# A decoder layer on one core: in the last group of the first attention, the bias, value and class products take earlier places in a hand-written order, and batch 1's middle stage moves up by 3.5 steps

## The reference, cut to what matters

```python
# first attention: classes of distance, 129 of them
dist = jnp.clip(idx[None, :] - idx[:, None], -R, R) + R        # R = 64
score = einsum('bhqd,bhkd->bhqk', q, k) + einsum('bhqd,qkd->bhqk', q, rel_emb_k[dist])
attn = softmax(score)
ctx = einsum('bhqk,bhkd->bhqd', attn, v) + einsum('bhqk,qkd->bhqd', attn, rel_emb_v[dist])
x = x + ctx @ W_out + b_out
x = x + memory_step(ctx_1024, layernorm(x))      # shifts, a convolution over 32 rows
# second attention and experts, on layernorm(x)
attn = softmax(rope(q) @ rope(k).T / sqrt(8));  x = rmsnorm(src + (attn @ v) @ Wo)
out = rmsnorm(x + shared + routed)
```

## Time and profile before

| | |
|---|---|
| time, median of 3 runs | 416.89 us (415.85 to 416.91) |
| the profiled execution: its time | 416.28 us |
| its span, first to last instruction | 414.5 us |
| mean granted TensorE clock | 0.916 |
| PE / DVE / ACT / POOL busy | 358.4 / 297.3 / 232.7 / 162.2 us |

### The profile page before, as it was taken

The page is one execution under the profiler, slowest core; times in us unless marked ns, Lnnn a source line. Parts: engine busy times, 40 slices in busy tenths (PEclk is TensorE's granted clock), DMA queues, the critical chain, the costliest instruction groups (busy, mean ns, idle before and its releaser), DMA issues.

```text
span 414.5 us, 12788 instructions
## 1 busy us (share of the span) xinstructions
PE 358.4 (86%) x5267; PEld 189.2 (46%) x5267; DVE 297.3 (72%) x538; ACT 232.7 (56%) x489; POOL 162.2 (39%) x342
## 2 busy tenths in 40 slices
PE   7776889898999999897889898768989898899993
PEld 4243456665676667664555332311233333453441
DVE  5996956777778788788799789566787661436465
ACT  2724665777676666665744567455767695422200
POOL 7263655465477576554470111200001161143423
PEclk9885558999999999999999699965999899999999
DMA  7400000000000001000000000500000000000000
GB/s 227 140 22 5 4 4 4 6 4 7 21 9 3 8 6 27 6 6 2 3 5 2 4 24 2 156 10 1 2 2 1 2 3 2 0 1 2 0 26 25
DMA packets 11991, 8.08 MB, mean 19 GB/s; under 512 B 4446, under 2 KB 11022, under 8 KB 11806
## 3 DMA queue, kind: packets, MB, share of 16 engines
q1 hardware_dynamic: 11934, 7.27, 6.1%
HBM read 5.94 MB, written 0.52 MB: 16 GB/s over the span
## 4 chain that ended last, share of the span: by engine, by line
PE 58%; DVE 21%; issue 7%; ACT 5%; SPq 3%; POOL 3%; DMA 2%; ACTq 0%; POOLq 0%; DVEq 0%
PE ps L1214 8%; PE ps L1309 7%; PE ps L1128 6%; PE ps L1159 5%; PE ps L1177 5%; PE ps L1186 4%; DVE m_qk L851 4%; PE ps L1201 4%; PE ps L1140 3%; PE ps L1004 3%; PE ps L1098 3%; DVE m_qk L848 2%; ACT arena L684 2%; PE ps L1295 2%; SPq L384 2%
## 5 line engine op out<-in xcount | busy, mean ns | idle before, releaser
L848 DVE TENSOR_REDUCE m_qk<-ps 128x2 f32<-128x1024 f32 x64 | 76.5, 1219 | 18.7 <-PE ps L1098 18.5
L851 DVE TENSOR_REDUCE m_qk<-ps 128x2 f32<-128x1024 f32 x64 | 76.9, 1219 | 16.1 <-PE ps L1186 15.7
L684 ACT ACTIVATE arena<-ps 128x512 f32<-128x512 f32 x128 | 69.4, 595 | 26.9 <-PE ps L1140 26.2
L699 ACT ACTIVATE arena<-ps 128x512 f32<-128x512 f32 x128 | 67.2, 591 | 21.3 <-PE ps L1201 21.0
L599 POOL TENSOR_TENSOR arena<-arena,eb 128x256 f32<-128x256 f32 x64 | 46.9, 733 | 60.6 <-ACT arena L684 31.5
L672 ACT ACTIVATE eb<-ps 128x512 f32<-128x512 f32 (+1 forms) x64 | 31.3, 542 | 28.0 <-PE ps L1128 28.0
L442 POOL TENSOR_SCALAR var<-mv 128x1 f32<-128x1 f32 (+1 forms) x14 | 2.7, 191 | 106.5 <-ACT eb L741 70.0
L1214 PE MATMUL ps<-arena,v_sb 128*20 128x256 f32 x512 | 41.2, 414 | 2.5 <-DVE arena L856 2.4
L1159 PE MATMUL ps<-arena,v_sb 128*20 128x128 f32 x1024 | 40.3, 284 | 0.0
L600 POOL TENSOR_TENSOR arena<-arena,eb 128x192 f32<-128x192 f32 x64 | 38.5, 602 | 0.0
L1201 PE MATMUL ps<-q_op,k_op 50*128 50x512 bf16 x128 | 31.9, 414 | 4.7 <-ACT arena L699 4.0
(11 more groups left out here) (217 smaller groups left out, 539.7 us busy)
## 6 DMA issues: line engine op xcount, KB each, us to landing
rel_v<-in_relv_ext SPq DMA_DIRECT2D x1, 1024.0 KB, 8.8
eb<-in_w SPq DMA_DIRECT2D x2, 512.0 KB, 5.6
x_sb<-in_x SPq DMA_DIRECT2D x2, 256.0 KB, 3.2
q_op<-farT SPq DMA_DIRECT2D x32, 3.0 KB
q_op<-farT SPq DMA_DIRECT2D x32, 1.5 KB
out<-x_sb SPq DMA_DIRECT2D x8, 64.0 KB, 1.5
rows<-in_rows SPq DMA_DIRECT2D x1, 448.0 KB, 6.6
sel<-in_sel SPq DMA_DIRECT2D x1, 384.0 KB, 4.2
```

What stands on the lines that cost most here:

```text
L684: act.activation(p_ring[:, k % SLOTS_P, e, :], ps[:, bank, :], ACT.Exp).then_inc(sm["bank_free"], 1)
L699: act.activation(p_ring[:, v % RING, e, :], ps[:, bank, :], ACT.Exp).then_inc(sm["bank_free"], 1)
L848: dve.tensor_reduce(m_qk[:, u, n:H:PAIRS], ps[:, banks, :], AX_X, ALU.max).then_inc(sm["pair_free"], 1)
L851: dve.tensor_reduce(m_qk[:, IT * b + n, 2 * p:2 * p + 2], ps[:, banks, :], AX_X, ALU.max).then_inc(sm["pair_free"], 1)
```

## The change

Only due times change; no instruction is added or removed, and the work of each item is as it was. For the last group (u = 7, start at step 84), `bias` items 1 to 3 come at 93.5, 95 and 96.5 in place of 95, 98 and 101; its eight `pv` at 106.5 to 110 in place of 108 to 112; its `crel` at 110.6 to 113 in place of 113 to 116; `ctx`, `turn`, `fin`, `norm`, `back` at 113.6, 114.2, 114.8, 116, 117.5 in place of 117, 117.6, 118.2, 119.5, 121. For the group before it (u = 6), `crel` comes at 102.3, 103, 103.7, 104.4 in place of 103 to 106, and `ctx` at 105.4 in place of 107. Batch 1's middle stage begins at 118.5 in place of 122, and its `max2` at 136 in place of 139. Batch 0's middle stage and its `max2` keep their times, as do `sc2`, `pv2` and all `scores`.

```diff
+BIAS_LAST = (8, 9.5, 11, 12.5)
+CREL_EARLY = (30.3, 31, 31.7, 32.4)
-PV_LAST = (24, 24, 25, 25, 26, 26, 28, 28)
-MID_AT = (78, 122)
-MAX2_AT = (102.6, 139)
+PV_LAST = (22.5, 22.5, 23.3, 23.3, 24.2, 24.2, 26, 26)
+CREL_LAST = (26.6, 27.4, 28.2, 29)
+MID_AT = (78, 118.5)
+MAX2_AT = (102.6, 136)
...
-        plan += [(t + (BIAS_AT if u else BIAS_FIRST)[q], 2, "bias", u, q) for q in range(4)]
+        bias_at, pv_at = (BIAS_LAST, PV_LAST) if u == NT - 1 else (BIAS_AT if u else BIAS_FIRST, PV_AT)
+        crel_at = CREL_AT if u < NT - 2 else (CREL_EARLY, CREL_LAST)[u - NT + 2]
+        plan += [(t + bias_at[q], 2, "bias", u, q) for q in range(4)]
         plan += [(t + SCORES_AT[p], 2, "scores", u, p) for p in range(PAIRS)]
-        pv_at, early = (PV_AT, 0) if u < NT - 1 else (PV_LAST, 2)
         plan += [(t + pv_at[k], 6, "pv", u, k) for k in range(8)]
-        plan += [(t + CREL_AT[q] - early, 7, "crel", u, q) for q in range(4)]
-        plan += [(t + 35 - early, 0, "ctx", u, 0)]
+        plan += [(t + crel_at[q], 7, "crel", u, q) for q in range(4)]
+        plan += [(t + crel_at[3] + (1 if u < NT - 2 else 0.6), 0, "ctx", u, 0)]
         if u == NT - 1:
-            plan += [(t + 33.6, 1.5, "turn", u, 0), (t + 34.2, 5, "fin", u, 0), (t + 35.5, 1.5, "norm", u, 0), (t + 37, 4, "back", u, 0)]
+            plan += [(t + 30.2, 1.5, "turn", u, 0), (t + 30.8, 5, "fin", u, 0), (t + 32, 1.5, "norm", u, 0), (t + 33.5, 4, "back", u, 0)]
```

## The result

| | before | after |
|---|---|---|
| time, median of 4 runs each | 416.90 us (415.85 to 418.85) | 426.77 us (423.58 to 427.60) |
| ratio | | 1.0217, 95% interval 1.0150 to 1.0284 |
| profiled execution: time, span, mean granted clock | 416.28, 414.5, 0.916 | 423.58, 421.8, 0.897 |

The change makes the kernel slower, by 1.5 to 2.8%. The profiled execution of the changed kernel lies 3.2 us under its median, that of the kernel before 0.6, so the two profiles show 7.3 of the 9.9 us between the medians; of the rest there is no trace.

What follows compares the result with a forecast made beforehand. No engine was always busy (PE nearest, 86%), so filling idle time decided. −3.95 to again1.6's end, +3.85 owed, −0.2 returned made −0.3: 416.0 us profiled, 416.6 as median; range 412.5 to 420.5.

Steps and rivals of the forecast that it cites:

- step 1: Batch 0's turns: bias7.1 ahead of proj0.0 costs PE 1.0 us, so again0.6 comes 1.0 us later, at 201.66.
- step 2: From again0.6 to crel7.3: crel7.3 starts 0.25 us sooner, with pv7.6 waiting 1.25 us.
- step 3: From crel7.3 to batch 1's y: 7.5 us in place of 8.5, y 1.25 us sooner, at 232.3.
- step 4: Batch 1 from y to xT: no change from 22.3 us, xT at 254.6.
- step 5: Batch 1 from xT to the end of again1.6: 2.7 us shorter, 24.4 in place of 27.1.
- step 6: Behind again1.6: four owed steps of max2, sc2 and pv2 cost 3.85 us; 0.2 comes back later.
- the prediction's own signs: Wrong if y before 230.5 or after 234, full clock behind the last again, or low clock past 243 us.
- group 7 comes late: Rival: pv7.6 waits 3 us for POOL's last multiplication, y no sooner; +1.75, 418.4 us; chance 0.12.
- the second rival: Lower clock lasts from y on, four more steps at 0.74 each, 3.0 us; 419.6 us; chance 0.17.
- The first rival: Holes in batch 1's middle stage close and the stretch behind stays at 2.4 GHz; 2.8 less, 413.8 us; chance 0.35.
- the upper end of the range: Whole time at most 420.5 us: the lower clock with one step more and a quarter of the POOL case.
- the least of the first rival: Smallest gain if holes close: pv7.6 not waiting (1.25) and DVE's sum short, giving 414.9 us.

Runs made afterwards that it cites:

- bias_only: Kernel before with only the last group's bias 1 to 3 at the new places; 419.73 us, ratio 1.0005.
- bias_behind: Kernel before with the last group's bias 1 left behind proj0.0, bias 2 and 3 sooner; 415.95 us, ratio 0.9958; again 419.23 us, 0.9978.
- change_bias_behind: Changed kernel with the last group's bias 1 behind proj0.0 and bias 2 and 3 later; 424.79 us, ratio 1.0128.
- fill_bank7: Changed kernel plus 19 idle 512-column matmuls into PSUM bank 7 from fin7 to the first pv2; 425.81 us, ratio 1.0138.
- after_again: Changed kernel itself, run and profiled a second time; 426.29 us, ratio 1.0254.
- crel6_late: Changed kernel with group 6's class products kept at 103 to 106, behind batch 0's first maxima; 427.16 us, ratio 1.0251.
- no_bias: Changed kernel without its bias part; 423.12 us, ratio 1.0117.
- fill_bias_behind: Changed kernel with 19 idle matmuls into bank 7 and bias 1 behind proj0.0; 418.64 us, ratio 1.0101.
- fill_again: Changed kernel with 19 idle matmuls into bank 7, run a second time; 422.90 us, ratio 1.0063.
- max_stay: Changed kernel with batch 1's maxima left at step 139; 422.54 us, ratio 1.0067.
- fill_bias_maxstay: Changed kernel with idle matmuls into bank 7, bias 1 behind proj0.0 and batch 1's maxima at 139; 418.09 us, ratio 1.0045.
- nobias_maxstay: Changed kernel without its bias part and with batch 1's maxima at 139; 426.15 us, no ratio.
- before_again: Kernel before, run and profiled a second time; 415.71 us, one run.

## Why the prediction was wrong, step by step

The marks of the changed kernel against those forecast, each stretch by itself: ahead of crel5.2 +1.6, step 1 +1.3, step 2 +0.5, step 3 +0.1, step 4 +2.2, step 5 +2.6, step 6 −0.7. Together the 7.6 us by which fin12 came later (358.7) than forecast (351.1). The first, +1.6, is no step of the sum: it lies in code that no edit touched. Of the prediction's own signs two came true: y at 235.7, after 234, and the clock low past 243.

**Step 1, the place of bias7.1: mis-sized.** I charged the item's own 1.0 us. It also holds a ring bank until ACT has taken its exponential, and scores6.5, now two items behind it, waits 0.56 us for that, a wait that I had put at nothing: crel5.2 to proj0.0 is 3.9 us in place of 2.3. bias_only carries this cost alone (24.2 against 22.8), and bias_behind and change_bias_behind are without it. 1.4 to 1.6 us at equal time at the lower level, taking A of fill_bank7 (23.5) and of before (21.9) for the upper. The rest of the 2.2 us by which A grew is 3.4 us at the lower level, which the kernel before has in one of its two profiles too. That the hole goes to back4 held, 2.01 us for 2.06.

**Step 2 held**: again0.6 to crel7.3 took 22.6 and, in after_again, 21.9 us, for 22.2 forecast. pv7.6 waited 1.08 for 1.25. **Step 3 held** in the first profile, 8.6 us from crel7.3 to y for 8.45; in after_again it was 9.1, with 5.1 us at the lower level. The rival "group 7 comes late" is out: POOL did end the group late (220.7, 40.3 us behind crel5.2's start, with the rival's point at 40.4), but PE was late by step 1 as well and waited no longer than summed, and crel6_late shows that the early crel6 helps.

**Step 4, y to xT "no change": wrong, and the clock is the cause.** The step counted items and DVE's waits and had no term for the clock. It took 24.5 and 24.3 us, with 7.5 and 10.6 at the lower level. With the idle matmuls it took 21.7, 0.6 under my sum, with none at the lower level: at full clock the count of items was right to 0.6. So the second rival had the right mechanism. I gave it 0.17 and 3.0 us, for four steps at one place; in the trace the falls come in pieces (one over y, another from 246.0 to 249.4), and again behind xT. The Trainium skill (TensorE: Matmul & The Clock Gate, HAM oscillation) says that idle gaps return the array to its throttled rate; the trace agrees, 1.00 granted with the gaps filled against 0.82 and 0.75 without.

**Step 5, 23.6 us from xT to the start of again1.6: wrong, 26.2.** The first half nearly held (15.0 to again1.0 for 14.8; 15.9 in after_again). From again1.0 to again1.6 it took 11.2 for 8.8, of which 9.7 at the lower level: an again had a length of 1.47 us there where I had counted 0.8, and the copies that the next one waits for begin only behind it. I laid this chain out at full clock though the row I had read just behind it ran at 0.59. Eight profiles have the order of the change there: 11.2 to 11.5 us with 9.4 to 9.7 at the lower level (after, after_again, crel6_late), 10.7 to 10.9 with 6.8 (no_bias, change_bias_behind, fill_bias_behind), 10.3 with 5.7 and 5.9 (fill_bank7, fill_again). A straight line through them comes to 8.9 with none, an estimate, and that is the 8.8 laid out. (max_stay took 8.7 with 3.4, but it has no maxima between the turns.) The first rival, holes that close, failed in its own terms: three more max2 between the projections did not lift the clock, and D had 12.6 and 15.0 us at the lower level, for 8.5 and 14.0 before.

**Step 6 held as a count.** What was owed came due: 72.2 us in E for 72.9 forecast, 69.9 and 67.7 before. It had been meant to be paid by steps 3 to 5, and 4 and 5 paid nothing.

Two small sums of the prediction are off, and nothing hangs on them: the upper end of the range, 419.6 with 0.74 for one step more and a quarter of 1.75, comes to 420.8 and not 420.5, and the least of the first rival, 1.25 and 0.76 under 416.6, to 414.6 and not 414.9.

**The size of each cause.** From crel5.2 on the change takes 178.3 and 179.0 us, the old order 172.6 and 172.3. The difference of the means is 6.2. Against the mean of 178.65 the idle matmuls take off 5.0 and 5.4, the later bias items 2.8, both together 6.2: they overlap (change_bias_behind also had 34.1 us at the lower level in place of 41.0 and 44.4). Together they are as large as the loss, but they are not its parts: with both, 20.5 us are at the lower level, where the kernel before has 27.3 and 30.7. The change has 13.7 us more there than the kernel before; at 0.24 to 0.29 us for each (worked out in the last section) that is 3.3 to 4.0 of the 6.2 us, an estimate. The bias place is 1.4 to 1.6. Some 1 us is left, which no run isolates; the maxima at 136 may be it, for fill_bias_maxstay takes 3.4 us less than fill_bias_behind with 6.8 us less at the lower level. Not settled either is why E of nobias_maxstay fell to the lower level, and by which rule the first 180 us vary.

## What to carry to other kernels

Where items are only reordered, count a moved item's buffer as well as its length: the next user of the ring waits for the reader of the one put ahead of it. Lay out every chain of dependent steps at both TensorE levels, and charge the lower one wherever the new order leaves TensorE waiting; a move that shortens idle on paper can lose more to the clock. And compare traces from the first moved item to the last, with the time at the lower level beside each stretch, before reading anything into the whole span.

## What the runs showed of the hardware that I had not expected

Runs of one and the same kernel differ by 3%, and the granted clock with them. Over all 98 executions of the kernel before, the time had a median of 417.3 and a spread from 411 to 424 us, and span and mean granted clock go together: spans of 409.3 us at 0.931, 415.3 at 0.912, 421.3 at 0.889. The code ahead of crel5.2 is the same in all versions (0 to about 180 us), and of that stretch three windows, from fill_again,

```profile
20.20:177.00 156.80, 138.08 (x3220) 93.72 (x3224) 120.75 (x209) 100.16 (x211) 92.97 (x171) 0.90 0.04 9
```

from before_again,

```profile
20.20:178.50 158.30, 139.93 (x3216) 94.50 (x3216) 121.33 (x209) 100.03 (x211) 92.88 (x171) 0.88 0.04 9
```

and from change_bias_behind,

```profile
20.70:186.00 165.30, 147.67 (x3221) 97.87 (x3224) 121.38 (x209) 100.67 (x211) 92.86 (x171) 0.82 0.04 9
```

show the same instructions, DVE, ACT and POOL busy alike, and 156.8, 158.3 and 165.3 us at 0.90, 0.88 and 0.82. To crel5.2 it is 30.7, 37.5 and 61.4 us at the lower level and 177.0, 178.5 and 186.0 us: (186.0 − 177.0) / (61.4 − 30.7) = 0.29 us lost for each us there, though a matmul takes twice as long there (y 2.08 against 1.05). A TensorE that never waited would lose 0.5 us for each; I take the rest for time in which it would have waited for another engine anyway, which no run shows by itself. The idle matmuls give nearly the same price: 5.2 us for 22.2 us fewer at the lower level, 0.24 each (means of two profiles each). The standard deviation of those 98 times is 3.1 us, so the median of four runs says little below 1%.
